# Down-weight butterflies spread over more steps, scale vectors computed on GpSimd, queries evicted before later statistics

## What is computed

```
# attention: 32 query heads, 8 key/value heads, head size 16
q, k, v = xn @ Wq, xn @ Wk, xn @ Wv
attn = softmax(q k^T * 16**-0.5);  s = (attn v) @ Wo
# feed-forward: fwht is a normalised Walsh-Hadamard transform over the last dimension
x = fwht(xn * SU_ug) / 64
up, gate = x @ W_up.T * (Wscale_ug[:2048] * 64), x @ W_gate.T * (Wscale_ug[2048:] * 64)
x = fwht(silu(gate) * up * SU_dp) / 64
g = x @ W_down.T * (Wscale_dp * 64)
```

## Time and profile before

| | |
|---|---|
| time, median of 3 runs | 1524.98 us (1524.01 to 1525.74) |
| the profiled execution's own time | 1525.26 us |
| its span, first to last instruction | 1523.5 us |
| PE busy | 1365.2 us, 90% |
| DVE busy | 1120.9 us, 74% |
| ACT busy | 724.5 us, 48% |
| POOL busy | 517.7 us, 34% |
| mean granted clock of TensorE | 0.975 |

### The profile page before, as it was taken

One profiled execution on the slowest core, in us unless ns is written; L12 is line 12 of the kernel. 1 busy time (PEld: TensorE's weight loads), 2 busy tenths in 40 slices (PEclk: granted clock), 3 DMA queues, 4 the chain that ended last, 5 costly groups with the idle time before them and its releaser, 6 DMA issues. The chain is left out here.

```text
span 1523.5 us, 24300 instructions
## 1 busy us (share of the span) xinstructions
PE 1365.2 (90%) x8972; PEld 662.7 (43%) x8972; DVE 1120.9 (74%) x1880; ACT 724.5 (48%) x1277; POOL 517.7 (34%) x426
## 2 busy tenths in 40 slices
PE   5878899999999999999798889988899888998887
PEld 2322333333333333333354366543765437654375
DVE  6878977787878777888367956769567785586854
ACT  4664666566655665665554222641225412264121
POOL 2599821022102210222145331452314523155231
PEclk9988999999999999999999999999999999999999
DMA  6420000100010001005502030020310203102121
GB/s 219 159 77 2 6 8 5 34 25 5 10 34 26 5 10 33 26 1 206 190 22 53 6 79 29 15 54 19 66 36 8 53 21 63 36 7 54 27 31 42
DMA packets 79573, 68.51 MB, mean 45 GB/s; under 512 B 45952, under 2 KB 67168, under 8 KB 76896
## 3 DMA queue, kind: packets, MB, share of 16 engines
q1 hardware_dynamic: 79456, 66.96, 14.9%
HBM read 44.87 MB, written 17.87 MB: 41 GB/s over the span
## 5 line engine op out<-in xcount | busy, mean ns | idle before, releaser
L599 DVE TENSOR_REDUCE mS<-bank 128x1 f16<-128x512 f32 x512 | 328.8, 684 | 123.6 <-PE bank L1105 121.7
L917 ACT ACTIVATE probs<-bank 128x512 f16<-128x512 f32 x512 | 277.2, 595 | 163.3 <-PE bank L1112 163.1
L1159 PE MATMUL bank<-rows,both 128*128 128x512 f16 x1024 | 242.9, 380 | 1.1 <-DVE th L628 1.1
L408 POOL TENSOR_TENSOR h<-th,h 128x512 f16<-128x512 f32 x58 | 68.0, 1172 | 235.4 <-ACT h L888 235.4
L2099 PE MATMUL fbank<-both,hid 128*128 128x512 f16 x512 | 122.9, 403 | 24.6 <-DVE hid L1646 24.6
L1159 PEld LDWEIGHTS bank<-rows,both 128*128 128x128 f16 x1024 | 91.4, 98 | 122.3 <-issue 15.8
L2083 PE MATMUL fbank<-rows,both 128*128 128x512 f16 x512 | 118.4, 385 | 4.7 <-ACT hid L1904 4.7
L2067 PE MATMUL abank<-rows,both 128*128 128x512 f16 (+1 forms) x480 | 113.0, 387 | 5.7 <-PEq L149 5.7
L1105 PE MATMUL bank<-qk 32*128 32x512 f16 x512 | 100.7, 388 | 18.6 <-DVE mS L599 8.6
L1112 PE MATMUL bank<-qv,qk 32*128 32x512 f16 x512 | 100.1, 388 | 0.0
L1173 PE MATMUL bank<-dn,h 128*128 128x512 f16 x256 | 98.4, 384 | 0.0
(11 more groups left out here) (292 smaller groups left out, 2658.2 us busy)
## 6 DMA issues: line engine op xcount, KB each, us to landing
h<-in_ug SPq DMA_DIRECT2D x8, 1024.0 KB, 5.0
lt_scratch<-big SPq DMA_DIRECT2D x16, 384.0 KB, 2.7
dn<-in_down SPq DMA_DIRECT2D x2, 2048.0 KB, 11.2
x_scratch<-th SPq DMA_DIRECT2D x16, 256.0 KB, 2.1
res<-x_scratch SPq DMA_DIRECT2D x16, 256.0 KB, 3.6
out_x<-res SPq DMA_DIRECT2D x16, 256.0 KB, 2.0
both<-in_w SPq DMA_DIRECT2D x2, 1548.0 KB, 10.1
t_scratch<-tok SPq DMA_DIRECT2D x8, 384.0 KB, 3.6
```

The lines of the kernel that those rows point to most:

```text
L408: pool.tensor_tensor(h16(ft, 1), row32, h16(ft, 0), ALU.subtract).then_inc(S["row_lo"], 1)
L599: v.tensor_reduce(mS[:, u % 2, qt, 32 * j + DH:32 * j + DH + 1], SA[n % 2][:, :], AX.X, ALU.max).then_inc(S["max_done"], 1)
L917: a.activation(probs[:, n % (2 * G), :], SB[n % 2][:, :], ACT.Exp, scale=float(DH) ** -0.5).then_inc(S["p_ready"], 1)
L1159: mm = pe.matmul(GB[n % 2][:, :], w[:, kt, col:col + P], xnb(b, kt), start=r == 0, stop=r == 2 * KT - 1)
```

## The change

- `DN_PAIR_AT`: pairs are placed later and further apart. 3 stand ahead of chunk 6 and 5 ahead of chunk 7; then one a step from 25 to 40, and one every second step from 41 to 61. `DN_AT`: the transforms start at step 49 and end at 68, where they were at 46 to 67.
- The scale vectors `usc`, `hsc` and `sudn` are computed by POOL, in five small instructions at steps 30 and 32, behind that step's pair. DVE keeps the scalars (`half_scale`, and two one-column instructions in place of the sixteen-column one of `bound_scales`). ACT's first tanh waits for two of POOL's five, DVE's first `up_mul` for four, ACT's first `high_down` for all.
- `LOW_FIRST` goes from 6 to 3: three `low_rows` move from DVE to POOL.
- In DVE's steps 1 and 2, `low_half` stands ahead of the statistics of batch 3.
- On ACT before step 0, `evict_q` stands ahead of `deviations(2)`, and `evict_v` ahead of `normalise(1)`.

```diff
-DN_AT = (46, 47, 51, 52, 53, 55, 57, 58, 59, 60, 61, 62, 63, 65, 66, 67)
-DN_PAIR_AT = (15, 15, 17, 17, 18, 19, 21, 21, 22, 23) + tuple(range(25, 46)) + (47,)
+DN_AT = (49, 51, 52, 53, 55, 57, 58, 59, 60, 61, 62, 63, 65, 66, 67, 68)
+DN_PAIR_AT = (16, 18, 19, 22, 23) + tuple(range(25, 41)) + tuple(range(41, 62, 2))
-LOW_FIRST = 6
+LOW_FIRST = 3
-        gsc = sb("gsc", [P, FT], F32)
+        gsc = usc[:, FT:UG]
+            def gate_scales():
+                pool.wait_ge(S["pow_a"], 2 * NCH + 3)
+                pool.tensor_tensor(usc[:, :].rearrange("p (c n) -> p c n", c=NCH), wsc[:, :].rearrange("p (c n) -> p c n", c=NCH),
+                                   powr[:, 1:1 + NCH].rearrange("p (c n) -> p c n", n=1).to_broadcast([P, NCH, UG // NCH]),
+                                   ALU.mult).then_inc(S["sc_ready"], 1)
+                pool.wait_ge(S["sc_ready"], 1)
+                pool.wait_ge(S["sc_half"], 1)
+                pool.tensor_tensor(usc[:, :], usc[:, :], top[:, 4:5].to_broadcast([P, UG]), ALU.mult).then_inc(S["sc_ready"], 1)
+                pool.wait_ge(S["sc_ready"], 2)
+                pool.tensor_tensor(hsc[:, :], usc[:, 0:FT], usc[:, FT:UG], ALU.mult).then_inc(S["sc_ready"], 1)
+
+            def product_scales():
+                pool.wait_ge(S["top_a"], 11)
+                pool.wait_ge(S["sc_ready"], 3)
+                pool.tensor_tensor(hsc[:, :], hsc[:, :], topr[:, 0:1].to_broadcast([P, FT]), ALU.mult).then_inc(S["sc_ready"], 1)
+                pool.tensor_tensor(sudn[:, :], sud[:, :], topr[:, 1:2].to_broadcast([P, FT]), ALU.mult).then_inc(S["sc_ready"], 1)
...
                 for k in range(len(DN_STEPS)):
                     if DN_PAIR_AT[k] == t:
                         dn_pair(k)
+                if t == 30:
+                    gate_scales()
+                if t == 32:
+                    product_scales()
...
                 v.wait_ge(S["top_a"], 9)
-                v.tensor_scalar(sudn[:, :], sud[:, :], topi[:, 1:2], DOWN_TOP * float(INTER) ** -0.5, ALU.mult, ALU.mult).then_inc(S["top_a"], 1)
+                v.tensor_scalar(topr[:, 0:1], topi[:, 0:1], ROW_TOP / D, None, ALU.mult).then_inc(S["top_a"], 1)
+                v.tensor_scalar(topr[:, 1:2], topi[:, 1:2], DOWN_TOP * float(INTER) ** -0.5, None, ALU.mult).then_inc(S["top_a"], 1)
...
-            def gate_scales():
...
-            def up_scales():
...
+            def half_scale():
+                v.tensor_scalar(top[:, 4:5], powr[:, 0:1], 0.5 * float(D) ** -0.5 / SUM_RAISE, None, ALU.mult).then_inc(S["sc_half"], 1)
...
-                    v.wait_ge(S["sc_ready"], 5)
+                    v.wait_ge(S["sc_ready"], 4)
...
+                if 0 <= t - PREP - 3 < NCH * KT:
+                    low_half(t - PREP - 3)
                 if t == 1:
                     statistics(3)
                 if t == 2:
                     inverse_deviations(3)
-                if 0 <= t - PREP - 3 < NCH * KT:
-                    low_half(t - PREP - 3)
...
                 if t == 29:
-                    gate_scales()
+                    half_scale()
                 if t == 30:
                     bound_scales()
-                if t == 31:
-                    up_scales()
...
                 if j == 0:
-                    a.wait_ge(S["top_a"], 10)
+                    a.wait_ge(S["sc_ready"], 5)
...
                 if b == 0 and ft == 0:
-                    a.wait_ge(S["sc_ready"], 5)
+                    a.wait_ge(S["sc_ready"], 2)
...
             evict_k(0)
+            evict_q(0)
             deviations(2)
-            evict_q(0)
             a.wait_ge(S["init"], 4)
+            evict_v(0)
             normalise(1)
-            evict_v(0)
             normalise(2)
```

More of the change, by code:

```diff
@@ L247, in layer0 @@
             "stats", "mvr", "sd_ready", "rs_ready", "nmr_ready", "xn_ready",
-            "amax_ready", "amax_all", "pow_a", "pow_b", "suc_ready", "bf1", "ug_hi_ready", "sc_ready", "dbf", "dn_abs", "dn_sum", "wmax", "wmax_all", "top_in", "top_a", "dn_hi", "row_full", "row_hi", "row_lo",
+            "amax_ready", "amax_all", "pow_a", "pow_b", "suc_ready", "bf1", "ug_hi_ready", "sc_ready", "sc_half", "dbf", "dn_abs", "dn_sum", "wmax", "wmax_all", "top_in", "top_a", "dn_hi", "row_full", "row_hi", "row_lo",
             "init", "slots_set", "heads_in0", "heads_in1", "heads_in2", "heads_in3",
@@ L578, in low_half @@
                                        ALU.mult, ALU.subtract).then_inc(S["gb_took"], 1)
-            def gate_scales():
[L581 to L588, removed]
-            def up_scales():
-                v.wait_ge(S["sc_ready"], 4)
-                v.tensor_scalar(hsc[:, :], hsc[:, :], topi[:, 0:1], ROW_TOP / (2 * D), ALU.mult, ALU.mult).then_inc(S["sc_ready"], 1)
+            def half_scale():
+                v.tensor_scalar(top[:, 4:5], powr[:, 0:1], 0.5 * float(D) ** -0.5 / SUM_RAISE, None, ALU.mult).then_inc(S["sc_half"], 1)
             def row_max(n):
```

## The result

The median is **1511.27 us** (1508.01 to 1516.0, 4 runs) against 1525.36 (1524.01 to 1526.44) of before: ratio 0.9911, 95% interval 0.9882 to 0.9939, so 14 us faster. The forecast was 1508.1, the range 1503.5 to 1515. After's profiled execution is its slowest: 1516.0, span 1514.2, against 1523.5 of before. Most of what follows is read there.

A forecast was written before the change was run, and what follows sets the result against it. PE sets the pace from 200 to 700 us, but the opening has about 20 us without its work. Terms 2.8 + 8.4 + 1.5 + 2.4 + 1.8 = 16.9 off 1525.26, less 0.3, give 1508.1 us, range 1503.5 to 1515.

The forecast's parts named there:

- Start: Before step 0: queries and values evicted earlier on ACT bring step 0 about 2.8 us sooner, bounds 0 and 3.5.
- Step 24: PE's wait of 7.02 us for POOL's chunk 6 and slow matmuls behind it go: 8.4 us, bounds 6.0 and 9.3.
- the lower bound's story: At step 24, a 1 us wait stays because PE comes sooner, and the clock still falls: 6.0 us gained.
- Step 28: PE's 1.29 us wait at chunk 7 and a little slow work go: 1.5 us, bounds 0.6 and 3.1.
- Scale vectors: Steps 29 to 31: moving them to POOL relieves DVE by 3.5 us net, 2.4 reaching PE, bounds 1.5 and 3.5.
- The hand-over: POOL's last vector for DVE's first `up_mul` ends at 137.9; the tightest place, with 0.3 us margin.
- The rival of a late POOL: POOL late at the hand-over, or PE slow in steps 27 to 32: 3 to 6 us less, about 1513; chance 0.22.
- The first tanh: On ACT, needs POOL's second vector only, two pairs or 5 us before `up_mul`'s, so called easier.
- Low rows: Steps 41 to 45: three leave full DVE for POOL, 1.8 us gained, bounds 0 and 2.5.
- Pairs and transforms moved back: Pairs in steps 41 to 61 fit POOL's idle time, moved transforms are neutral on PE: cost 0.
- The sum: All terms together, from start to low rows: 16.9 us gained.
- the rival of more clock: Fewer gaps keep PE at 2.4 GHz, steps 5 to 24 quicken: 3 to 5 us more, about 1504; chance 0.15.

The follow-up runs named there:

- e1: The kernel before with only the new order on ACT before step 0; 1521.68 us, ratio 0.998.
- f3: The changed kernel with the statistics of batch 3 ahead of `low_half` on DVE, as before; 1509.89 us, ratio 0.9905.
- e2: The kernel before with only the new `DN_AT` and `DN_PAIR_AT`; 1517.58 us, ratio 0.9944.
- f2: The changed kernel with `LOW_FIRST = 6`, six low rows on DVE as before; 1512.3 us, ratio 0.9916.
- g3: The changed kernel with `product_scales` called at step 34 instead of 32; 1513.14 us, ratio 0.9918.
- e3: The kernel before with only the scale vectors moved to POOL; 1527.56 us, ratio 1.0013.
- f1: The changed kernel with the old `DN_AT` and `DN_PAIR_AT`; 1522.15 us, ratio 0.9976.
- f4: The changed kernel with two pairs instead of three ahead of chunk 6; 1511.27 us, ratio 0.9898.
- g2: The changed kernel with DVE's inputs of the last sum split, only one column's square left behind the last chunk maximum; 1510.38 us, ratio 0.9905.
- g1: f4 with DVE's inputs of the last sum split, only one column's square left behind the last chunk maximum; 1510.58 us, ratio 0.9904.
- e4: The kernel before with only `LOW_FIRST = 3`, three low rows moved from DVE to POOL; 1530.4 us, ratio 1.0028.
- the last kernel: g1 without the POOL pairs of steps 29 and 30, later pairs moved back; 1506.38 us, ratio 0.9868.

## Why the prediction was right, point by point

- **Start**, 2.8 forecast: 3.1 in after, 2.1 alone in e1, 2.1 to 3.2 in all kernels with the new start. The mechanism is right, the size depends on when a load lands (e1). What holds step 0 next was named wrongly: not the head copies, but `evict_v` behind `deviations(2)` and DVE's statistics. The order on DVE was taken as 0 and is 0 (f3).
- **Step 24**, 8.4: the step itself gave 6.4, and 1.2 came in steps 20 to 23: 7.6. The 1.2 belongs to the spread. Before's clock was at 0.50 from 92.0 us for 3.4, in all five kernels with the old lists it falls at this place, and in none of the nine with new lists. The sum lies between the bounds 6.0 and 9.3, and the lower bound's story is what happened: the wait stays 0.91 us because PE comes sooner, and the clock falls behind it. In e2, f2, f3 and g3 the clock did not fall there, and step 24 gave 7.7 beside the 1.2.
- **Steps 25 to 27**, nothing forecast: 1.0 lost. This is the term that the working lacked. 0.3 of it is the end of the slow stretch of step 24, and 0.7 is step 27, where the square of eight columns takes 1.13 us instead of 0.47. With other lists it meets another POOL instruction: a long way from its end in after, shortly before its end in before. I had looked at what POOL makes late, not at what it makes slow.
- **Step 28**, 1.5: 1.2. The wait for POOL is gone, but clock and DVE (busy 4.29 of 4.40 us) hold the step.
- **Scale vectors**, 2.4: 2.4 in after, 2.8 in e3. The five vectors take 0.22 to 0.25 us each, 1.1 together against the 1.0 taken.
- **The hand-over.** The last vector was put at 137.9 on before's clock; it ended at 134.40, and 3.3 us of start added make it 137.7. POOL's sum was right. The margin was 2.8 us and not 0.3; 1.6 of that is the first `up_mul` itself, at 137.00 where 135.4 was forecast. It is not firm: 1.5 and 1.6 in f3 and f4, 0.2 in f2 and g2, nothing in g1, and it does not go by PE's lead alone (17.4 us at step 32 in f3, 15.5 in g2). The rival of a late POOL did not come about in after, but its mechanism is shown four times: in e3 and f1 (2.4 us), in g1 (2.4) and in g3 (3.6). The first tanh was called easier, by two pairs; in e3, f1 and g1 it is nevertheless released by POOL too, after 2.2 to 2.3 us of idle time, and goes before `up_mul`.
- **Low rows**, 1.8: 2.0 in after, 1.9 alone, 0.3 without them. The size is right, but it is not a property of the rows: in e2 the new lists alone gave 1.6 in the same steps (see f2).
- **Pairs and transforms moved back**, 0: no `up_mul` waits for L425. The transforms' move gains 1.8 us in steps 46 to 48 and loses 1.4 in step 49 and 0.9 in step 68, net -0.5. On PE a transform costs 0.9 to 1.0 us wherever it stands, as forecast; what was missed is 0.43 us that PE waits in step 49, ahead of the key projection. It waits for `low_down` (L650) on DVE, and that for ACT's high half of the same transform (L886):
```profile
178.57 0.70 ACT L886 ACTIVATE dn<-bank,sudn 128x512 f16<-128x512 f32 x1
179.31 0.75 DVE L650 SCALAR_TENSOR_TENSOR dn<-bank,sudn,dn 128x512 f16<-128x512 f32 x1 [0.82 <-ACT dn L886]
180.11 1.04 PE L1078 MATMUL bank<-rows,wk 128*128 128x512 f16 x4 [0.43 <-DVE dn L650]
```
- **The sum.** Layer 0 gave 15.4 us against 16.9 forecast; from step 12 on the parts alone give 9.9 + 0.9 + 1.9 = 12.7 and after 12.1, so they add up nearly. But part of the agreement is luck: f3, which does the same work, gained 18.8 in layer 0, 3.4 more, with 6.8 us at clock 0.50 there and not 17.1, and the forecast had that only as the rival of more clock, with a chance of 0.15. Behind step 255 after's profiled execution lost 6.1 us again, and shows 17.6 us more at clock 0.50. Over the fourteen kernels the length of that stretch rises with its time at 0.50, by 0.37 us for each us on a straight line through them, with up to 2 us of scatter at the same time: 829 to 831 us at 49 to 56, 833 to 839 at 63 to 70. After's four times have the same order: 1508.01, 1510.29, 1512.25 and 1516.0 at mean clocks of 0.980, 0.978, 0.975 and 0.972. The 3 us between forecast and median may be 1.5 of layer 0 and as much of clock; the median execution was not profiled, so that is not shown.

What stays open is why some kernels have the low clock more often in a stretch where they are the same, and whether the edits have a part in that. e4's 1530.4 and e3's 1527.56 are of this kind, their median clocks 0.971 and 0.973 against 0.977 of before, and no experiment here settles it.

The Trainium skill (SBUF — State Buffer, "SBUF: two separate sides") says that the shared port pair is held for the whole instruction, and that DVE needs it in a two-port mode, or with two SBUF inputs against a GpSimd instruction that reads SBUF. f4's and g1's rows agree: with two tensor inputs 2.25 us, ending with POOL's; one column with one tensor input and a scalar 0.21 under the same POOL instruction.

The Trainium skill (GPSIMD Engine Reference, "4.1 Engine selection") spoke against moving `low_rows`, with GpSimd about twice as slow for two inputs. The traces agree with it roughly where POOL is idle: 0.67 us on DVE in e2 against 1.16 on POOL, 1.7 times. Beside POOL's pairs the three left on DVE took 1.39 on average in after, and what decided was that DVE was full: the move gains.

## What to carry to other kernels

When a queue is relieved so that a consumer comes earlier, list every hand-over that this engine makes afterwards with its margin in us; here the margin of the first `up_mul` was 2.8 us and then below zero, and the last kernel was found by it. DVE's instructions with two tensor inputs, small ones too, are better placed where POOL is idle or a step ahead of their use. One column with one tensor input was spared (0.21 us in g1), but that form alone is no safeguard: before's L585 with 32 columns has one tensor input as well and took 1.18 us. And book the gain by stage before comparing medians: parts of 2 us can be read in the stage's own rows where the granted clock is the same, while the totals of equal code differ by 8 us with it.

## What the runs showed of the hardware that was not expected

- A DVE product of seven or eight columns took 0.16 to 2.25 us, by what POOL did beside it (0.16 with seven columns in g1, 0.28 in e3, 0.47 in before, 1.13 in after, 1.50 in e2, 2.25 in f4).
- A `low_rows` of 512 columns took 0.67 us on DVE with POOL idle (e2) and 1.16 to 1.74 beside POOL's pairs in after, where each ended 0.55 us behind the POOL instruction that it had met; on POOL it takes 1.16.
- On POOL a product of 16 or 32 columns takes 0.21 to 0.25 us.
- The clock fell to 0.50 for 3.4 or 6.8 us after short waits of PE in some executions and not in others: behind the same wait of 0.91 us in after (1.91 us for the pair of matmuls) and not in e2 (1.10 for the first).
